# Two cross-attentions over 257 keys: head sums by batch on VectorE, the output projection a slot later, the key copy before the own-head product

## The reference, cut to what matters

```python
q = layernorm_per_head(h @ Wq)         # L1; in L2 plain, with biases
k = layernorm_per_head(ctx @ Wk)       # L1; in L2 plain, with biases
s = einsum("bhqd,bhkd->bhqk", q, k)    # 32 queries by 257 keys, L2 adds a mask
p = softmax(s)
o = einsum("bhqk,bhkd->bqhd", p, ctx @ Wv)
x = x + o.reshape(B, 32, 128) @ Wo + bo
```

## Time and profile before

| | us |
|---|---|
| median of 3 runs | 3913.97 (3908.17 to 3917.47) |
| the profiled execution | 3910.4 |
| its span, first to last instruction | 3908.6 |
| busy in the span: PE, DVE, ACT, POOL | 2978.2, 2481.4, 2048.3, 1967.2 |
| mean granted TensorE clock | 0.887 of full speed |
| L1's attention, first to last scores | 818.3 to 1269.0 |
| L2's attention, first to last scores | 1840.2 to 2366.4 |
| maxima of one score block (L2660), mean | 0.418 |
| exponential of one score block (L2622), mean | 0.475 |
| head sum of four batches (L2682), mean | 1.050 |

### The profile page before, as it was taken

One profiled execution on the slowest core, in us unless ns is written; L12 is line 12 of the kernel. 1 busy time (PEld: TensorE's weight loads), 2 busy tenths in 40 slices (PEclk: granted clock), 3 DMA queues, 4 the chain that ended last, 5 costly groups with the idle time before them and its releaser, 6 DMA issues. The chain is left out here.

```text
span 3908.6 us, 79627 instructions
## 1 busy us (share of the span) xinstructions
PE 2978.2 (76%) x23619; PEld 2035.7 (52%) x23619; DVE 2481.4 (63%) x6469; ACT 2048.3 (52%) x6345; POOL 1967.2 (50%) x1964
## 2 busy tenths in 40 slices
PE   6969586778888597585999995888862558858957
PEld 4759434456666485453666663333322336735645
DVE  6856686667777573343777775989875213447862
ACT  5535405567777454233666664545431124548953
POOL 4630205667777693062565654888860441116720
PEclk9979798989999798797999998999985778978978
DMA  3300002322222000111111112434331127900000
GB/s 99 88 25 0 6 1 68 97 66 73 75 75 71 8 2 6 57 47 44 31 32 31 32 31 67 148 134 140 137 112 62 27 44 201 215 6 3 2 7 22
DMA packets 138838, 233.70 MB, mean 60 GB/s; under 512 B 28652, under 2 KB 100623, under 8 KB 137848
## 3 DMA queue, kind: packets, MB, share of 16 engines
q1 hardware_dynamic: 130488, 221.61, 19.4%
q0 software_dynamic: 8128, 9.45, 1.4%
HBM read 200.44 MB, written 13.71 MB: 55 GB/s over the span
## 5 line engine op out<-in xcount | busy, mean ns | idle before, releaser
L2433 POOL TENSOR_TENSOR l2x_att_prob<-l2x_att_prob,l2x_att_rs 128x1024 f32<-128x1024 f32 x128 | 242.5, 1895 | 214.1 <-DVE l2x_att_rs L2665 214.1
L3202 PE MATMUL l2a_pY<-l2a_hc,ident 128*128 128x512 f32 x512 | 273.2, 672 | 91.4 <-POOL l2a_hc L3121 57.0
L2433 POOL TENSOR_TENSOR l1x_att_prob<-l1x_att_prob,l1x_att_rs 128x1024 f32<-128x1024 f32 x128 | 242.6, 1895 | 136.8 <-DVE l1x_att_rs L2665 136.8
L3091 POOL TENSOR_TENSOR l2a_dbu<-l2a_dx,l2a_BC 128x1024 f32<-128x1024 f32 x128 | 298.6, 2354 | 20.7 <-PE l2a_pY L3202 10.6
L2622 ACT ACTIVATE l2x_att_prob<-l2x_att_pS,l2x_att_nmx 128x257 f32<-128x257 f32 x512 | 236.3, 475 | 115.4 <-DVE l2x_att_nmx L2660 115.4
L2622 ACT ACTIVATE l1x_att_prob<-l1x_att_pS,l1x_att_nmx 128x257 f32<-128x257 f32 x512 | 236.3, 475 | 102.9 <-DVE l1x_att_nmx L2660 102.8
L3219 ACT ACTIVATE l2a_pA<-l2a_dl,l2a_A 128x512 f32<-128x512 f32 x256 | 174.6, 689 | 187.7 <-DVE l2a_pH L3325 112.7
L2660 DVE TENSOR_REDUCE l2x_att_nmx<-l2x_att_pS 128x1 f32<-128x257 f32 x512 | 182.0, 418 | 110.3 <-PE l2x_att_pS L2537 110.3
L3325 DVE TENSOR_TENSOR_SCAN l2a_pH<-l2a_pA,l2a_dbu 128x512 f32<-128x512 f32 x192 | 224.8, 1217 | 23.4 <-POOL l2a_dbu L3091 12.3
L2660 DVE TENSOR_REDUCE l1x_att_nmx<-l1x_att_pS 128x1 f32<-128x257 f32 x512 | 182.0, 418 | 85.7 <-PE l1x_att_pS L2532 85.7
L3202 PEld LDWEIGHTS l2a_pY<-l2a_hc,ident 128*128 128x128 f32 x512 | 103.5, 211 | 252.6 <-issue 119.4
(11 more groups left out here) (741 smaller groups left out, 8988.2 us busy)
## 6 DMA issues: line engine op xcount, KB each, us to landing
l2a_BC<-l2a_rows SPq DMA_DIRECT2D x128, 512.0 KB, 3.8
l3x_att_ctn<-ctx_n SPq DMA_DIRECT2D x32, 576.0 KB, 14.3
l0x_att_kvs<-ctx_t SPq DMA_DIRECT2D x32, 514.0 KB, 3.5
l1x_k_xin<-ctx_t SPq DMA_DIRECT2D x32, 514.0 KB, 3.5
l1x_att_ctx<-ctx_t SPq DMA_DIRECT2D x128, 128.5 KB, 2.1
l1x_att_kT<-l1x_KA SPq DMA_DIRECT2D x128, 128.5 KB, 2.2
l2x_att_ctx<-ctx_t SPq DMA_DIRECT2D x128, 128.5 KB, 2.1
l3x_att_ctx<-ctx_t SPq DMA_DIRECT2D x32, 514.0 KB, 12.5
```

The lines of the kernel that those rows point to most:

```text
L2433: pool.tensor_tensor(p, p, bc(rs[:, b, :], 2, LAST), ALU.mult).then_inc(scaled, 1)
L3091: pool.tensor_tensor(dbu[:, u % 3], dx[:, g % 2], bc(BC[:, u % RING, 0, :], 1, NC), ALU.mult).then_inc(dbu_made, 1)
L3202: last = pe.matmul(pY[c][:, :], env.ident[:, :], hc[:, u % 3, c, :], start=False, stop=n == NS - 1)
```

## The change

Five edits in `cross_attention`, effective in both attentions:

1. `own` shrinks from four batches with the batch inside to two buffers of one batch, `[P, 2, R, S]`; `own_head` writes `own[:, b % 2]`.
2. `sum_heads` runs in every slot, for one batch, and writes its 32 columns of `osum`; it stands last in VectorE's slot. `osum_made` counts batches, so `output` waits for `made(4 * g + 3)`.
3. `output(k - 1)` moves on TensorE from the end of slot c = 1 to slot c = 2, behind `attend` and ahead of the keys' product.
4. `keys` (L2 only) moves on VectorE ahead of `own_head`, right behind the maxima.
5. `add` moves on VectorE within slot c = 2 from ahead of the maxima to behind `own_head`; `attend` waits for `added` in the slot of b == 1 in place of b == 0; `own_head` of b == 0 waits for `out_made` of the group before in place of `osum_made`.

```diff
@@
-        own = st.sb("own", [P, R, BT, S])
+        own = st.sb("own", [P, 2, R, S])
@@ attend
-                    if b == 0:
+                    if b == 1:
                         after(pe, added, k - 1)
@@ output
-                    pe.wait_ge(osum_made, made(g))
+                    pe.wait_ge(osum_made, made(4 * g + 3))
@@ slot of TensorE
                     if c == 1 and inside(n - 5):
                         turn_tails()
+                    if c == 2 and inside(n - 6):
+                        output(k - 1)
                     if inside(n + 2) and KA is None:
                         keys(n + 2, c, k)
...
                         values(n + 2, c, k)
-                    if c == 1 and inside(n - 5):
-                        output(k - 1)
-
@@ VectorE
-                def sum_heads(k):
-                    dve.wait_ge(own_made, made(4 * k + 3))
-                    after(dve, out_made, k - 1)
-                    dve.tensor_reduce(osum[:, :, :].rearrange("p b q -> p (b q)"),
-                                      own[:, :, :, :].rearrange("p h b q -> p (b q) h"), AX.X, ALU.add
+                def sum_heads(n, b):
+                    dve.wait_ge(own_made, made(n))
+                    dve.tensor_reduce(osum[:, b, :], own[:, b % 2].rearrange("p h q -> p q h"), AX.X, ALU.add
                                       ).then_inc(osum_made, 1)
@@ own_head
                     if b == 0:
-                        after(dve, osum_made, k - 1)
+                        after(dve, out_made, k - 1)
...
-                        dve.scalar_tensor_tensor(out=own[:, :, b, :], in0=o, scalar=cols[:, 1:2], in1=m, op0=ALU.add,
+                        dve.scalar_tensor_tensor(out=own[:, b % 2], in0=o, scalar=cols[:, 1:2], in1=m, op0=ALU.add,
                                                  op1=ALU.mult).then_inc(own_made, 1)
                     else:
-                        dve.tensor_tensor(own[:, :, b, :], o, m, ALU.mult).then_inc(own_made, 1)
+                        dve.tensor_tensor(own[:, b % 2], o, m, ALU.mult).then_inc(own_made, 1)
@@ slot of VectorE
                     if inside(n):
                         factors(n, c)
-                    if c == 2 and inside(n - 6):
-                        add(k - 1)
                     if inside(n + 1):
                         maxima(n + 1, (c + 1) % 4)
+                    if inside(n + 2) and KA is None:
+                        keys(n + 2, c)
                     if inside(n - 2):
                         own_head(n - 2, (c - 2) % 4, k if c >= 2 else k - 1)
                     if c == 1 and inside(n - 5):
                         keep_tails(k - 1)
-                        sum_heads(k - 1)
-                    if inside(n + 2) and KA is None:
-                        keys(n + 2, c)
+                    if c == 2 and inside(n - 6):
+                        add(k - 1)
                     if inside(n - 1):
                         keep_turned(n - 1, (c - 1) % 4)
+                    if inside(n - 2):
+                        sum_heads(n - 2, (c - 2) % 4)
```

## The result

The changed kernel takes 3816.9 us in the median of four executions (3814.13 to 3826.46), the kernel before 3911.6 beside it (3908.17 to 3917.47): a ratio of 0.9749 with a 95% interval of 0.9715 to 0.9783. In a second series, of six executions, it was 0.9756 (0.9727 to 0.9785). The forecast was 3817.

The account below looks back on a forecast made before the run. Dependency rings and TensorE's order bound the two attentions, with the long sum, projection and late keys' copy lengthening slots. Savings of 27 us (l1x) and 67 us (l2x), -94 in all, gave 3817 us, range 3801 to 3849.

Parts of the forecast that it names:

- The gap in slot 1, l1x: First attention: sum and projection leave slot 1, 4.25 to 3.33 us, -0.92; slot 2 pays +0.07; stage -27 us.
- l2x's cadence: Second attention: TensorE's own order sets most slots; group 14.47 us against 16.62, -2.15; stage -67 us.
- Slot 0: Second attention, slot with last-keys product: 3.64 us, -0.38; keys' copy ends at 2.69, before the turn at 2.80.
- The floor of slot 3: Second attention, slot 3: 3.41 us as read at the stage's start, -0.31, instead of TensorE's own 3.34.
- the ring of keys and exponentials: Second attention: the recurring dependency through keys' copy and exponentials, taken to keep slot 3 at 3.41 us.
- The cover: VectorE, both attentions: short sums of 360 ns each cost nothing, hidden in idle time; some 0.3 us left in l2x.
- The waits that were added: Own-head product's wait for projection taken as 0; projection's wait for fourth sum has 0.8 to 1.0 us margin; addition over 1.
- A: Rival, second attention: TensorE's busy 15.08 of 16.62 us is the floor; -48 in place of -67, 3837 us; chance 0.22.
- B: Rival: projection and wait lengthen slot 2 in full, 0.64 in l1x, 0.54 in l2x; 3844 us; chance 0.12.
- C: Rival: short sums do not shrink and VectorE becomes the bound; at 1.5 us each, 3992 us; chance 0.03.
- D: Rival: the wait for the sum only moves to the projection in slot 2; 3911 us; chance 0.03.
- The other stages: Sign outside the two edited attentions: the prediction is wrong if any other stage changes its length.

Follow-up runs that it names:

- The kernel with the keys behind: Changed kernel with VectorE copying the keys behind the own-head product and tails again; ratio 0.9824 to the kernel before, l2x group 15.25 us.
- an earlier start of the scores: Changed kernel with scores waiting for the exponentials in two steps, blocks 0 to 2 after the third, block 3 after all four; ratio 0.9726 to the kernel before.
- the late long sum: Changed kernel with one sum of four batches again, at the end of VectorE's slot 1, projection still in slot 2; ratio 0.9768 to the kernel before.
- the doubled sums: Changed kernel with each batch's sum done twice, the first into a spare tile nothing reads; ratio 0.9771 to the kernel before.

## Why the prediction was right

The mechanism was right: the sum and the projection left slot 1, the copy of the keys moved ahead, and both stages shortened as forecast, l1x by 30.2 us (27 forecast) and l2x by 67.3 (67 forecast). That 3817 meets the median to 0.1 us is luck: the stages gave 97.5 us where 94 were forecast, the medians differ by 94.7 only, and in l2x errors of up to 0.15 us per slot cancel. Point by point:

- **The gap in slot 1, l1x.** -0.92 for slot 1 was forecast, -0.94 measured. Slot 2 was charged +0.07 for the projection and paid nothing. The 0.64 of the projection was taken from a place ahead of the scores (0.32 + 0.32, and the row at 1013.90 that they leave out); ahead of the turn it is 0.55 (1011.89 to 1012.44), and the turn behind it takes 0.88 in place of 0.93. So slot 2 still ends with ScalarE.
- **l2x's cadence.** The slots are off by -0.15, +0.06, +0.12 and -0.07, and the errors cancel in the sum (14.47 against 14.42). The turn was taken at 0.93 from l1x, where it follows the attend or the tails; in l2x it follows the keys' matmul and takes 0.88, with no wait in either place. That is nearly all of the error of slot 1, and a part of the others. In slot 2 the keys' matmul also takes 0.43 behind the projection (2060.72 to 2061.15) and not the 0.54 that it takes behind the attend.
- **Slot 0.** 1.06 us pass from the turn to the last-keys product (2053.47 to 2054.53) where I counted 0.93. The step that failed is the comparison of the copy's end, 2.69, with the turn's, 2.80: this product starts some 0.24 us behind the copy's end in both kernels, so the copy still sets slot 0. The kernel with the keys behind bears this out: the copy 0.26 us later there made slot 0 0.26 longer (3.76 to 4.02).
- **The floor of slot 3.** I read 3.41 from the stage's start as the ring of keys and exponentials. In the changed kernel slot 3 is 3.47. The copy of the keys is at its edge there, as the values' row of 0.71 us shows; an earlier start of the scores took 0.04 off. The number was usable; which of the two holds the slot was not shown by a run.
- **The cover.** The sum takes 356 to 376 ns, 360 were assumed. It's hidden, with 0.17 us to spare ahead of the maxima in l2x where some 0.3 were forecast. "The scaling is needed a whole slot later" left out that the queries stand behind the scaling on GpSimd, and that the next scores read them: the late long sum and the doubled sums both show this path, and not the maxima, as the first to give way. The earlier trace rows is also not the only reduction over groups of eight: L377 takes 420 ns for 256 elements to 32 outputs, a nearer bound from above than 485.
- **The waits that were added.** The own-head product's wait for the projection, the addition behind it and the projection's wait for the fourth sum cost nothing, as forecast.
- **The rivals.** A (TensorE's busy rows as a floor of 15.08) fell: the group is 14.43, and the busy rows shrank with it. The Trainium skill (Perfetto Trace Analysis, Identifying the Most-Contended Engine) says that matmul busy time is a poor gauge of headroom; this trace agrees, 15.08 us of busy rows became 14.41 for the same matmuls. One of the gauges that the page offers instead, the weight loads, doesn't tell the bound here: 11.02 of 14.43 us, in a stage where TensorE has next to no idle time left. B (slot 2 pays in full) fell in l1x by its whole 0.6, and in l2x partly: slot 2 is 3.73 with the projection and 3.41 without it, +0.32 of 0.55. C and D did not occur.
- **The other stages.** A change of length in them was named as a sign against the forecast. They did move, by 13.6 us in all between the two profiles, but they also differ between profiles of kernels that are equal there: behind l2x it was 1550 us in both profiles of the changed kernel, 1542 in the kernel before, and 1554 with only the keys' copy moved.

Of the 97.5 us, per group 0.96 in l1x and 2.20 in l2x. Taken away from the changed kernel one at a time, the place of the projection is worth 0.87 and 0.95, the place of the keys' copy 0 and 0.83, the split of the sum 0.19 and 0.19. The parts overlap, and so don't add up: alone, the copy's place gives 1.13, and with the projection in its old place the split gives 0.69 in both stages where the short sums stand ahead of the turned copy.

## What to carry to other kernels

Look for what stands between the last input of a ring and the instruction that closes it, on either engine's in-order queue: a product that nobody needs soon, issued ahead of the scores, cost l1x 0.9 us in a slot of 3.3, and moving it behind the scores made it free. Order each engine's slot by who waits longest for what: the copy that another engine needs first, then the work whose readers come a slot later. What splitting a long instruction is worth depends on its place: 0.69 us per group where another engine waits for it and the last piece stands first, 0.1 to 0.2 in the other orders that were run. And follow every output of a delayed instruction: the reciprocal behind the sum feeds the maxima's engine and GpSimd, and it was GpSimd's next piece of work that held the scores.

## What the runs showed of the hardware

- What a group of matmuls takes from its start to the next start depends on its neighbours, and is the same to 0.01 us with and without waits around it. The eight transposes of a turn take 0.93 us behind products on parts of the array (attend, 128*32, or tails, 32*32) and 0.87 to 0.88 behind products of 128*128; the keys' matmul 0.54 and 0.44; the second half of the projection 0.22 ahead of another product of 128*128 and 0.32 ahead of the scores (32*128). A duration has to be read where the neighbours are those of the new order.
- Rows of busy time overlap more when waits go: in l2x 15.08 us per group became 14.41 for the same matmuls.
- VectorE's sum over groups of four costs more for its size than one over longer groups: 512 elements to 128 outputs take 1050 ns, 128 elements to 32 outputs 364, over a third. That is 7.1 ns per output of four elements; 256 elements in groups of eight to 32 outputs (L377) take 420.
- A VectorE instruction that waits for the one right ahead of it starts 0.11 us later than one that doesn't (0.37 and 0.26 us).
